# Expert stage of an audio tower: six shared chunks behind the routed blocks, ten pair buffers, both pair additions on GpSimd

## The reference, cut to what matters

```python
hs = gelu(einsum('td,nfd->ntf', t, sw1) + sb1)            # two shared experts, 512 hidden each
shared = einsum('ntf,ndf->td', hs, sw2) + sb2.sum(0)
probs = softmax(t @ gate_w.T + gate_b)                    # eight routed experts
top_v, top_i = top_k(probs, 2)
hr = gelu(einsum('td,efd->etf', t, rw1) + rb1)
routed = sum over the two chosen experts of top_v * (hr @ rw2.T + rb2)
h = h + shared + routed
```

## Time and profile before

| what | value |
|---|---|
| median of 3 runs | 2655.36 us |
| lowest and highest run | 2651.74 and 2657.29 us |
| span of the profiled execution | 2655.1 us |
| time of the profiled execution besides its span | not given |
| busy share of PE, PEld, DVE, ACT, POOL | 90%, 69%, 76%, 63%, 42% |
| mean granted TensorE clock, of full speed | 0.942 |

### The profile page before, as it was taken

How to read it: one execution, slowest core, us unless ns; L and a number is a source line. 1 busy time by engine, 2 the same in 40 slices (tenths; PEclk the granted TensorE clock), 3 DMA queues, 4 the chain that set the end, 5 groups by cost and what they waited for, 6 DMA issues and landing times. The chain is left out here.

```text
span 2655.1 us, 52098 instructions
## 1 busy us (share of the span) xinstructions
PE 2389.5 (90%) x16443; PEld 1819.7 (69%) x16443; DVE 2026.5 (76%) x3647; ACT 1665.8 (63%) x3127; POOL 1124.6 (42%) x1338
## 2 busy tenths in 40 slices
PE   7989699999999999854899997999849999999993
PEld 7989455444445444343799997888738887888882
DVE  4555589999999999489688887788776666787775
ACT  3345267777777777743566664555527777777772
POOL 0016002223223222323777773444337774666664
PEclk9999699999999999975899998999969999999997
DMA  3108633333333323054111112400021113777749
GB/s 90 36 12 319 193 56 50 62 62 56 48 62 62 57 47 62 18 152 149 42 38 38 39 38 68 164 0 0 1 81 52 51 52 103 243 240 247 243 143 277
DMA packets 161298, 249.19 MB, mean 94 GB/s; under 512 B 41645, under 2 KB 106902, under 8 KB 154233
## 3 DMA queue, kind: packets, MB, share of 16 engines
q1 hardware_dynamic: 128888, 208.77, 29.1%
q0 software_dynamic: 19712, 38.13, 4.9%
q10 hardware_dynamic: 12544, 0.39, 0.2%
HBM read 155.24 MB, written 93.41 MB: 94 GB/s over the span
## 5 line engine op out<-in xcount | busy, mean ns | idle before, releaser
L1014 ACT ACTIVATE probs<-score 128x748 f32<-128x748 f32 (+1 forms) x768 | 568.4, 794 | 117.2 <-PE score L839 115.8
L943 DVE TENSOR_REDUCE part_max<-to_dve 128x1 f32<-128x512 f32 (+1 forms) x768 | 479.7, 683 | 84.0 <-PE to_dve L820 83.6
L2762 DVE TENSOR_TENSOR m_hid_lo<-m_up,m_hid_hi 128x512 fp32r<-128x512 f32 x408 | 279.9, 687 | 157.1 <-ACT m_hid_hi L2735 157.1
L820 PE MATMUL to_dve<-k_stack,q_stack 48*128 48x512 f32 (+3 forms) x1536 | 351.4, 367 | 20.9 <-DMA k_stack<-k_parts 20.1
L839 PE MATMUL score<-q_stack,k_stack 49*128 49x374 f32 (+1 forms) x1536 | 317.3, 389 | 3.1 <-ACT probs L1014 1.0
L839 PEld LDWEIGHTS score<-q_stack,k_stack 49*128 49x128 f32 (+1 forms) x1536 | 162.0, 181 | 225.0 <-ACT probs L1014 199.7
L876 PE MATMUL o_sum<-probs,v_sb 128*17 128x374 f32 (+1 forms) x3072 | 315.6, 483 | 0.1
L2658 POOL DMA_INDIRECT e_sums<-m_gated,m_row_in x216 | 212.6, 984 | 162.3 <-DVE m_gated L2780 109.2
L820 PEld LDWEIGHTS to_dve<-k_stack,q_stack 48*128 48x128 f32 (+1 forms) x1536 | 223.1, 187 | 79.7 <-DVE part_max L943 36.6
L740 POOL TENSOR_TENSOR o_rows<-o_raw,inverse 128x384 f32<-128x384 f32 x32 | 26.9, 842 | 589.7 <-DVE inverse L953 589.7
L1371 POOL DMA_INDIRECT f_row_in_c<-c_rows,c_ids x192 | 218.4, 1137 | 75.2 <-issue 49.6
(11 more groups left out here) (411 smaller groups left out, 6003.8 us busy)
## 6 DMA issues: line engine op xcount, KB each, us to landing
m_weights<-e_records SPq DMA_DIRECT2D x54, 1028.0 KB, 6.9
q_stack<-q_parts SPq DMA_DIRECT2D x192, 93.5 KB, 3.1
k_stack<-k_parts SPq DMA_DIRECT2D x192, 93.5 KB, 4.2
e_slots<-blank SPq DMA_DIRECT2D x54, 260.0 KB, 3.9
m_row_in<-e_slots SPq DMA_DIRECT2D x54, 260.0 KB, 3.3
m_weights<-e_sums SPq DMA_DIRECT2D x16, 640.0 KB
e_records<-l_parts SPq DMA_DIRECT2D x16, 512.0 KB, 3.7
v_rows<-v_out SPq DMA_DIRECT2D x16, 408.0 KB, 5.9
```

Of the source, the lines that this page charges most:

```text
L820: last = pe.matmul(ring[i % RING][0:ROWS[c], at_col:at_col + keys.stop - keys.start], q_stack[its_slot][rows, j, c * P:c * P + ROWS[c]], k ...
L943: dve.tensor_reduce(part_max[0:ROWS[c], k, j, c, 0:1], ring[i % RING][0:ROWS[c], :], AX.X, ALU.max).then_inc(used, 1)
L1014: act.activation(probs[0:n, s % 2, m, 2 * j:2 * j + 2, :], score[tile][0:n, :, 0:HALF], ACT.Exp).then_inc(tile_used, 1)
L2762: dve.tensor_tensor(hid_lo[:, f % RING, :], up[f % UPS][:, :], hid_hi[:, f % RING, :].bitcast(F32), ALU.subtract).then_inc(lo_done, 1)
```

## The change

`EARLY` goes from 21 to 18, so six shared chunks, not three, stand behind the routed blocks. A scatter asks for 38/50 of a step in place of 43/50. The pair buffers go from 4 to 10: the six new ones lie in `rows`, in the 72 tiles that the 18 early chunks read. The second addition of a pair moves from VectorE to GpSimd, where it waits for the first; `add_pair` and `LATE` are gone.

```diff
-    EARLY = 21
+    EARLY = 18
...
-    LATE = starts[shared_at[EARLY]] + 10
+    SPARE = EARLY * SUB // (2 * TILES)
+    PAIRS = WEIGHTS + SPARE
...
-    assert (TOP * N - 1) * 43 // 50 - SLACK <= starts[routed_at[0]] - TURN - LAG
+    assert (TOP * N - 1) * 38 // 50 - SLACK <= starts[routed_at[0]] - TURN - LAG
...
-        pair_in = [sem(f"pair_in{k}") for k in range(WEIGHTS)]
+        pair_in = [sem(f"pair_in{k}") for k in range(PAIRS)]
...
         def pair_of(b):
-            return weights[:, b % WEIGHTS, 0:TILES * TOP * P].bitcast(F32).rearrange("p (c k d) -> p c k d", c=TILES, k=TOP)
+            s = b % PAIRS
+            if s < WEIGHTS:
+                flat = weights[:, s, 0:TILES * TOP * P].bitcast(F32)
+            else:
+                flat = rows[:, (s - WEIGHTS) * 2 * TILES:(s - WEIGHTS + 1) * 2 * TILES, :].rearrange(
+                    "p n r -> p (n r)")[:, 0:TILES * TOP * P]
+            return flat.rearrange("p (c k d) -> p c k d", c=TILES, k=TOP)
...
-                    if b >= WEIGHTS:
-                        sp.wait_ge(added, b - WEIGHTS + 1)
+                    if b >= PAIRS:
+                        sp.wait_ge(added, b - PAIRS + 1)
...
-                for b in range(WEIGHTS):
+                for b in range(PAIRS):
                     fetch_pair(b)
                 for b in range(B):
                     store(b)
-                    if b + WEIGHTS < B:
-                        fetch_pair(b + WEIGHTS)
+                    if b + PAIRS < B:
+                        fetch_pair(b + PAIRS)
...
-                        steps_asked = (k * N + n) * 43 // 50 - SLACK
+                        steps_asked = (k * N + n) * 38 // 50 - SLACK
...
                 for b in range(B):
-                    pool.wait_ge(pair_in[b % WEIGHTS], 32 * (b // WEIGHTS + 1))
+                    pool.wait_ge(pair_in[b % PAIRS], 32 * (b // PAIRS + 1))
                     pool.wait_ge(returned, shared_at[((b + 1) * TILES - 1) // SUB] + 1)
                     h = g.h[:, b * TILES:(b + 1) * TILES, :]
                     pool.tensor_tensor(h, h, pair_of(b)[:, :, 0, :], ALU.add).then_inc(summed, 1)
+                    pool.wait_ge(summed, b + 1)
+                    pool.tensor_tensor(h, h, pair_of(b)[:, :, 1, :], ALU.add).then_inc(added, 1)
...
-                def add_pair(b):
-                    dve.wait_ge(summed, b + 1)
-                    h = g.h[:, b * TILES:(b + 1) * TILES, :]
-                    dve.tensor_tensor(h, h, pair_of(b)[:, :, 1, :], ALU.add).then_inc(added, 1)
...
-                    if f >= LATE and (f - LATE) % 2 == 0:
-                        add_pair((f - LATE) // 2)
...
-                for b in range((ENDS - LATE + 1) // 2, B):
-                    add_pair(b)
```

More of the change, by code:

```diff
@@ L2607, in fetch_pair @@
                     first, whole = b * TILES * P * TOP, (TILES - 1) * P * TOP
-                    if b >= WEIGHTS:
-                        sp.wait_ge(added, b - WEIGHTS + 1)
+                    if b >= PAIRS:
+                        sp.wait_ge(added, b - PAIRS + 1)
                     sp.dma_start(pair_of(b)[:, 0:TILES - 1, :, :].rearrange("p c k d -> p c (k d)"),
                                  sums[first:first + whole, :].rearrange("(c p k) d -> p c (k d)", p=P, k=TOP)
-                                 ).then_inc(pair_in[b % WEIGHTS], 16)
+                                 ).then_inc(pair_in[b % PAIRS], 16)
                     sp.dma_start(pair_of(b)[0:LAST, TILES - 1, :, :].rearrange("p k d -> p (k d)"),
                                  sums[first + whole:first + whole + LAST * TOP, :].rearrange("(p k) d -> p (k d)", k=TOP)
-                                 ).then_inc(pair_in[b % WEIGHTS], 16)
+                                 ).then_inc(pair_in[b % PAIRS], 16)
                 def store(b):
```

## The result

| | median, us | runs | range, us | ratio to before, 95% interval |
|---|---|---|---|---|
| before | 2654.55 | 8 | 2651.74 to 2657.29 | |
| after | 2662.46 | 8 | 2659.4 to 2664.87 | 1.0028 [1.0019, 1.0037] |

The change makes the kernel 7.9 us slower; 8.1 us more were forecast. The profiled execution of after has a span of 2659.2 us and took 2660.96, 1.8 us more than its span and 1.5 less than the median of its runs. If as much lies around the span of before, that execution took 2656.9, which is 2.3 over its median. So the two spans differ by 4.1 us and the medians by 7.9: the page of before came from one of the longer executions, that of after from one of the shorter ones.

The account below looks back on a forecast made before the run. GpSimd's scatters were taken to bound the start of routed work, and GpSimd's additions the changed tail: 2596.4 + 60.8 + 5.7 + 0.3 = 2663.2 us, 2663.4 on the median, range 2656 to 2671.

Parts of the forecast that it names:

- Asked steps: Scatters of token rows: asking for fewer steps gains and loses nothing; the scatters still end near 2213.
- Three chunks moved: Before the routed blocks: TensorE comes 35.6 us earlier and idles 38.5 us; routed work still starts at 2217.67.
- Clock: Routed restart after the longer idle time: extra loss between 0 and 1.3 us, taken as 0.7.
- First addition: Tail: the first pair's sum keeps its place behind the routed blocks, 2595.67 before, 2596.4 with the clock's 0.7 us.
- Ten pair buffers: Tail: loads are hidden with some 12 us in hand; without the buffers GpSimd would wait for pairs.
- Additions: GpSimd in the tail: 1.82 us each, bounds 1.47 and 2.05; 3.80 us a batch, 60.8 us for 16.
- The end: Last store's issue to span end: 5.7 us as before, plus 0.3 for clearing six more semaphores.
- Who ends last: Tail: GpSimd comes to batch 15 at 2653.4, TensorE's last chunk is back at 2649.4; GpSimd last by 4 us.
- TensorE last: Rival for the tail: batches under 3.53 us let TensorE end last, median 2658.8, +0.13%; chance 0.20.
- additions slowed by VectorE: Rival for the tail: GpSimd's additions take 2.05 us each, median 2670.8; chance 0.12.
- paced scatters: Rival: the asks paced the scatters, which end up to 28 us sooner, median about 2635; chance 0.03.
- The first rival: TensorE ends last and the change costs nothing measurable, if a batch takes less than 3.53 us; chance 0.20.

Follow-up runs that it names:

- ask38: The kernel before with one edit, a scatter asking for 38/50 of a step in place of 43/50: 2655.89 us, ratio 0.9995.
- four_buffers: The kernel after with four pair buffers in place of ten: 2661.66 us, ratio 1.0026 to before.
- one_add: The kernel after with the second addition of each pair left out: 2659.82 us, ratio 1.0012 to before.
- dve_second: The kernel after with the second addition back on VectorE, one in two late steps from the 18th on: 2667.03 us, ratio 1.0036 to before.
- early21: The kernel after with 21 early chunks again and so 11 pair buffers: 2662.59 us, ratio 1.0022 to before.
- buffers11: The kernel before with eleven pair buffers and nothing else: 2654.45 us, ratio 1.0001.
- split_adds: The kernel after with 21 early chunks, 11 buffers, both additions of batches 0 to 9 on GpSimd, 10 to 15 on VectorE: 2655.80 us, ratio 1.0004 to before.

## Why the prediction was right, step by step

| step | forecast | measured in after |
|---|---|---|
| last scatter ends | near 2213, unmoved | 2212.83 |
| TensorE's idle time in front of the routed blocks | 38.5 us | 37.80 |
| loss of clock by the longer idle time | 0.7 us | none in this pair; 0.5 on average over all profiles |
| first addition starts | 2596.4 | 2593.48 |
| 16 batches on GpSimd | 60.8 us | 59.7 |
| store asked to the end of the span | 6.0 us | 6.0 |
| end of the span | 2663.2 | 2659.2 |

*Asked steps.* Right: shown by `ask38`.

*Three chunks moved.* Right: 35.6 us of cover became idle time of TensorE, and the start of the routed work did not move. From the first scatter to the first routed turn are 249.3 us on average over the five profiles with 21 early chunks and 249.2 over the four with 18.

*Clock.* The stretch from 2216 is at 0.50 and the one from 2220 at 0.65, about as in the earlier trace rows. From the routed turn to the first late product the five profiles with 21 chunks average 353.8 us and the four with 18 chunks 354.3: 0.5 us for 38 us of idle time in place of 2 to 3. The single profiles overlap (353.56 to 354.10 with 21, 353.96 to 354.74 with 18), so the size is uncertain and its sign only likely.

*First addition.* Here the sum was 2.9 us too late. 0.7 is the clock, and 0.7 that this execution came to the routed turn sooner. Most of the rest is the landing of the last sums: the first load is asked for 3.5 us behind the start of the last scatter before, 2.2 us after. The forecast kept this term as it was, and that is wrong: the five profiles with 21 early chunks have 3.08 to 3.52 us, the four with 18 have 2.22 to 2.24. With this, the first load stands 621.75 us behind the first scatter with 21 early chunks and 621.1 with 18: where 0.7 us later was forecast, 0.6 sooner came. So on average 1.3 of the 2.9 us belongs to the change, 1.1 of it in this landing; the rest is how these two executions fell.

*Ten pair buffers.* That loads are hidden is right. That GpSimd would wait for pairs without the six new buffers, as it does before, is wrong: `four_buffers` shows one wait, for the first pair. It is the slower pace of GpSimd, 3.73 us a batch, that hides the loads.

*Additions.* The chosen 1.82 us was low by up to 0.06 while VectorE runs (mostly 1.84 to 1.88, and 1.80 once it is done), and the gaps were taken 0.13 too long a batch: 3.73 us in place of 3.80. Neither bound came near: not 1.47, the form with a repeated operand, and not 2.05, the form beside a VectorE addition. The estimate of 1.69 us from the Trainium skill (GPSIMD Engine Reference, section 3.1) is 0.1 to 0.2 low, and the measured rows decide. Its section 4.1, that two-input elementwise work belongs on VectorE, agrees with the rows here, 1.80 against 0.95 us.

*The end.* 39 semaphores to clear: 5.71 and 5.76 us from the last store's issue to the end (before, `ask38`) and 5.78 in `four_buffers`; 45: 6.01, 6.09 and 6.06 (after, `one_add`, `dve_second`); 46: 6.09 (`early21`). The 0.3 us is there. `buffers11` (46) and `split_adds` (48) take 6.56 and 7.12 us, but there the DMA engines are still full when the last store is asked for.

*Who ends last.* Right, but closer than worked out: 1.8 us between GpSimd and the late chunks in place of 4.0.

The rivals fell: TensorE last (`early21`), additions slowed by VectorE (no addition over 1.88 us), paced scatters (`ask38`). Of the signs that were named, three came a little off: the first late product (2570.97, where 2572 to 2573 was said), the row of additions (2593 to 2653, where 2596 to 2657 was said) and the longest addition (1.88 us, where 1.86 was said). The first rival has a true core: by the 1.8 us it would have decided below 3.61 us a batch (3.73 less 1.8 / 15) where 3.53 was worked out, and `one_add` shows what it would have cost.

How close the number came is in part luck. Against the profile of after the sum is 4.0 us too long, 2.9 for the first addition and 1.1 for the batches; the medians agree with it to 0.2 us, but the interval of the ratio runs from 5 to 10 us, and the level of before itself moves by 2.5 us between sets. What the runs bear out is the mechanism and a loss of that order.

The change gains nothing, because TensorE's waits for VectorE in the tail of before, which it does take away, were not what ended that kernel: with TensorE done 12 us sooner (`split_adds` against `buffers11`) the end is level.

## What to carry to other kernels

Before work is moved behind a stage to fill an idle engine, ask which resource fills that stage: here DMA set 64 us of tail, so an idle TensorE there was free of charge and filling it gained nothing, while the stage that the work came from, paced by GpSimd's scatters, did not get shorter. An addition moved to a slower engine is priced by its row times its count in a line, 16 x 3.73 us, against the floor it stands beside: here 70.7 us from the first load to the end, where loads and stores alone need 63 to 65. When the chain of waits names an engine, look whether another works beside it without a gap; moving the named one away, as `early21` does, tells the two apart.

## What the runs showed of the hardware that was not expected

VectorE and GpSimd, both adding two operands from SBUF, fell into one rhythm in `split_adds`. GpSimd's timeline, then VectorE's:

```profile
2614.29 1.80 POOL L2677 TENSOR_TENSOR h<-h,e_rows 128x768 f32<-128x768 f32 x1
2616.17 1.80 POOL L2679 TENSOR_TENSOR h<-h,e_rows 128x768 f32<-128x768 f32 x1
2617.92 2.52 POOL L2677 TENSOR_TENSOR h<-h,e_rows 128x768 f32<-128x768 f32 x1
2620.52 2.40 POOL L2679 TENSOR_TENSOR h<-h,e_rows 128x768 f32<-128x768 f32 x1
```

```profile
2616.49 2.28 DVE L2815 TENSOR_TENSOR h<-h,e_rows 128x768 f32<-128x768 f32 x1 [6.71 <-DMA e_rows<-e_sums]
2618.81 2.44 DVE L2817 TENSOR_TENSOR h<-h,e_rows 128x768 f32<-128x768 f32 x1
2621.18 2.55 DVE L2815 TENSOR_TENSOR h<-h,m_weights 128x768 f32<-128x768 f32 x1
...
2633.67 0.96 DVE L2817 TENSOR_TENSOR h<-h,m_weights 128x768 f32<-128x768 f32 x1
```

Each addition takes about 2.45 us on either engine, where alone they take 1.80 and 0.95: starts follow one another by 2.4 to 2.6 us on both sides. The Trainium skill (SBUF — State Buffer, section "SBUF: two separate sides") describes the pair of ports that the two share as an exclusive lock for a whole instruction; by that, two engines in turn would need 1.80 + 0.95 = 2.75 us a round. The trace is 0.3 us below.

The landing of the last sums took two lengths, from the chain of waits of `early21` and of `four_buffers`:

```profile
2589.48 3.36 DMA e_sums<-m_gated,m_row_in
```

```profile
2589.64 2.09 DMA e_sums<-m_gated,m_row_in
```

The two lengths go with one thing in the profile's DMA view. In all five kernels with 21 early chunks one load of the instruction queue (0.02 MB) is moved about 1 us behind the start of the last scatter, and the first load of a pair is asked for 3.08 to 3.52 us behind that start. In the four with 18 none falls near it, and the load is asked for 2.22 to 2.24 us behind. The bandwidth of `split_adds` from 2570 to 2600, in slices of 0.75 us, has it as the 22 at 2585, behind the scatter that starts at 2584.07:

```profile
GB/s 0 0 1 0 1 0 1 0 0 1 0 1 0 1 0 1 0 1 0 1 22 0 0 0 78 131 362 385 348 352 348 320 335 358 324 340 380 372 381 344
```

Whether the load is what lengthens the landing was not tried.
